# The recurrent unit's input is turned, copied and split ahead of a window of the graph step instead of behind it

## The reference, cut to what matters

```python
msg = h[edge_src] + relvectors[edge_rel]
red = jax.ops.segment_sum(msg, edge_dst, num_segments=h.shape[0])
gi = red @ w_ih.T + b_ih
gh = h @ w_hh.T + b_hh
r = sigmoid(i_r + h_r);  z = sigmoid(i_z + h_z)
n = tanh(i_n + r * h_n)
new = (1.0 - z) * n + z * h
```

## Time and profile before

| | us |
|---|---|
| Median of 3 runs | 3483.4 |
| Lowest and highest | 3481.09, 3487.05 |
| The profiled execution, whole | 3481.69 |
| Its span, first to last instruction | 3480.1 |
| First layer's windows and steps | about 160 to 1620 of the span |
| Mean granted PE clock, share of 2.4 GHz | 0.781 |

### The profile page before, as it was taken

The page is one execution under the profiler, slowest core; times in us unless marked ns, Lnnn a source line. Parts: engine busy times, 40 slices in busy tenths (PEclk is TensorE's granted clock), DMA queues, the critical chain, the costliest instruction groups (busy, mean ns, idle before and its releaser), DMA issues. The chain is left out here.

```text
span 3480.1 us, 54363 instructions
## 1 busy us (share of the span) xinstructions
PE 2374.7 (68%) x13318; PEld 1809.5 (52%) x13319; DVE 1521.8 (44%) x3970; ACT 779.9 (22%) x1414; POOL 1854.4 (53%) x2044
## 2 busy tenths in 40 slices
PE   1278777778677777645577766555543799999991
PEld 1155454545455444524355544433322799999991
DVE  5543443443444443422466554432321454554545
ACT  1222222222222221202101100000000344454440
POOL 0263433443645676771777777777775344444440
PEclk7578788888888888756678766666655899999996
DMA  5331211211222233331433333333332222222116
GB/s 139 97 86 45 61 55 55 61 57 52 85 73 77 79 107 98 100 104 34 114 114 115 113 108 108 108 110 106 106 107 78 86 68 65 68 66 64 45 44 230
DMA packets 157909, 303.68 MB, mean 87 GB/s; under 512 B 47365, under 2 KB 91816, under 8 KB 157752
## 3 DMA queue, kind: packets, MB, share of 16 engines
q0 software_dynamic: 85984, 234.74, 23.2%
q1 hardware_dynamic: 40876, 36.11, 3.4%
q10 hardware_dynamic: 30892, 31.40, 2.8%
HBM read 261.73 MB, written 40.39 MB: 87 GB/s over the span
## 5 line engine op out<-in xcount | busy, mean ns | idle before, releaser
L743 POOL DMA_INDIRECT rows<-table,srcT x1568 | 1552.8, 990 | 910.1 <-issue 463.1
L811 PE MATMUL bank<-rows,onehot 128*128 x3904 | 700.2, 330 | 537.6 <-POOLq L736 403.1
L811 PEld LDWEIGHTS bank<-rows,onehot 128*128 x3904 | 427.4, 109 | 801.4 <-issue 653.5
L772 DVE SCALAR_TENSOR_TENSOR onehot<-iota_row,tbase,dstT 128x512 f16 x488 | 366.2, 752 | 625.9 <-issue 332.9
L1752 PE MATMUL bank<-xe_high,W_high 128*128 128x256 f32 x864 | 252.0, 292 | 30.2 <-DVE xe_low L1830 29.9
L1802 ACT ACTIVATE hid<-bank,b 128x256 f32<-128x256 f32 x432 | 181.2, 471 | 345.6 <-PE bank L1754 345.5
L1838 DVE TENSOR_TENSOR hid_low<-hid,hid_high 128x512 fp32r<-128x512 f32 x216 | 149.6, 693 | 234.4 <-ACT hid_high L1806 234.4
L1753 PE MATMUL bank<-xe_low,W_high 128*128 128x256 f32 x864 | 250.2, 290 | 0.0
L1754 PE MATMUL bank<-xe_high,W_low 128*128 128x256 f32 x864 | 249.9, 289 | 0.0
L1752 PE MATMUL bank<-W_high,hid_high 128*128 128x256 f32 x864 | 248.4, 287 | 0.0
L1754 PE MATMUL bank<-W_high,hid_low 128*128 128x256 f32 x864 | 244.0, 282 | 0.0
(11 more groups left out here) (338 smaller groups left out, 3598.3 us busy)
## 6 DMA issues: line engine op xcount, KB each, us to landing
rows<-table,srcT POOLq DMA_INDIRECT x1568, 2.7
W<-in_L_ffn_W_dram SPq DMA_DIRECT2D x14, 1024.0 KB, 7.5
y<-results ACTq DMA_DIRECT2D x12, 1024.0 KB, 10.3
x_res<-in_x_dram SPq DMA_DIRECT2D x1, 6144.0 KB, 43.8
out_dram<-x_res SPq DMA_DIRECT2D x12, 512.0 KB
table<-part ACTq DMA_DIRECT2D x11, 512.0 KB, 3.2
normal<-xn ACTq DMA_DIRECT2D x11, 512.0 KB, 3.4
table<-part SPq DMA_DIRECT2D x6, 512.0 KB, 2.9
```

Of the source, the lines that this page charges most:

```text
L743: nc.gpsimd.indirect_dma_start(out=rows[:, k % (M * U), 0:ROW], out_offset=None, in_=q.table, in_offset=bass.IndirectOffsetOnAxis(srcT[:, ...
L772: last = nc.vector.scalar_tensor_tensor(onehot[:, ds(slot, U), :], iota_row[:, :].unsqueeze(1).to_broadcast([P, U, P]), base, dstT[:, ds(k ...
L811: last = nc.tensor.matmul(acc[:, 0:cols], hot, ring_rows[:, ds(row0 + (s * q.pitch + at), cols)], start=False, stop=False, skip_group_chec ...
```

## The change

The first three bullets of d1 move to the end of d4 of the group ahead, on each of the three engines. For group 0 they stay in d1. On PE the transposes stand behind the last L1012 and before window 3. On ACT the copies to `t_high` stand behind the last copy of d4 and before the square root. On DVE the subtraction stands behind the last L207 and before the one-hots. Nothing is added or removed: same instructions, tiles and semaphores. The copies to `hT` stay in d1.

```diff
-        def pe_d1(pe, g, w):
-            n = w * P
-
+        def pe_d0(pe, g, w):
             pe.wait_ge(S["h4_ready"], g + 1)
             for c in range(C):
                 for i in range(w):
                     last = nc.tensor.transpose(bank[c][:, i * P:(i + 1) * P], h4_in[:, i, c * P:(c + 1) * P], ident[:, :])
             last.then_inc(S["hT_ps"], 1)
+
+        def pe_d1(pe, g, w):
+            n = w * P
+
+            if isinstance(g, int) and g == 0:
+                pe_d0(pe, 0, w)
...
                 l3(a2_low, 1 + pair, eW3[0][:, pair, :], False, pair == 1)
-
-        def act_d1(act, g, w):
+            if not (isinstance(g, int) and g == LAST):
+                pe_d0(pe, g + 1, size(g + 1))
+
+        def act_d0(act, g, w):
             n = w * P
             act.wait_ge(S["hT_ps"], g + 1)
             for c in range(C):
                 last = nc.scalar.activation(t_high[:, c, 0:n], bank[c][:, 0:n], ACT.Copy)
             last.then_inc(S["hT_high"], 1)
...
+            if not (isinstance(g, int) and g == LAST):
+                act_d0(act, g + 1, size(g + 1))
             ln_sqrt(act, S["x2_var"], S["x2_std"], g, w, scaled=True)
...
             chain.begin(g)
-            dve_low(dve, g, w, t_low, t_high, 0, 1, "hT_high", "hT_low")
+            if isinstance(g, int) and g == 0:
+                dve_low(dve, 0, w, t_low, t_high, 0, 1, "hT_high", "hT_low")
...
             ln_apply(first_tile(g), w).then_inc(S["h2_ready"], 1)
             chain.end()
+            if not (isinstance(g, int) and g == LAST):
+                dve_low(dve, g + 1, size(g + 1), t_low, t_high, 0, 1, "hT_high", "hT_low")
```

More of the change, by code:

```diff
@@ L1040, in act_d1 @@
             last.then_inc(S["hT_high"], 1)
+        def act_d1(act, g, w):
+            n = w * P
+            if isinstance(g, int) and g == 0:
+                act_d0(act, 0, w)
             act.wait_ge(S["ct_ps"], g + 1)
```

## The result

The changed kernel takes 3440.2 us in the median of four runs (3435.27 to 3446.88), the kernel before 3484.2 us beside it. A second pair, further down, gives 0.9886 (0.9868 to 0.9904).

The account below looks back on a forecast made before the run. The chain of steps on PE, DVE and ACT, not POOL's gather, bounds groups 2 to 11. Per group 2.6 - 0.9 = 1.7 us, over ten groups 17 us, from 3483.4 to 3466 us; the range leaving out 2 in 10 is 3455 to 3479.

Parts of the forecast that it names:

- The root: ACT's copies stand before the square root at the end of d4: root 0.2 us late, bounds 0 and 0.9.
- that group's zero: Group 1, like groups 0, 12 and 13, was forecast to gain about zero.
- the clock's term: Products from instruction 10 in d1: half clock for 5 us after PE's wait, giving back 0.8 to 0.9 us a group.
- That gives back 0.8 to 0.9 us: In d1, the block from instruction 10 takes 16.8 us instead of 16.03, against 2.6 us gained before it.
- PE has then waited some 4.5 us in one piece: Ahead of instruction 10 in d1, PE's wait for `red_low` was to be as long as before the change.
- the hand-over: DVE's last one-hot to instruction 10 in d1(6): 5.35 us instead of 8.32, with 0.3 added for hand-overs and register work.
- the 0.4 that I had allowed: PE's transposes stand before window 3: PE reaches its first product at most 0.4 us later, range -0.7 to +0.4.
- The rule of the Trainium skill that I set against the change: Waits between bursts of matmuls put PE back to half clock, each burst paying anew; without it the sum would be 26 us.
- the clock stays full: Rival, chance 0.05: PE's ten products ahead of the wait keep the clock up; 4.05 us a group, 3443 us.
- The one-hots are held back: Rival, chance 0.15: DVE doesn't take the subtractions ahead, one-hots come 0.65 to 1.29 us later; 3474 us.
- slower: Rival, chance 0.08: register work starts only behind the subtraction, one-hots 2.31 us late; 1.4 us lost in ten groups, 3497 us.
- The gain is absorbed: Rival, chance 0.12: what follows d1 ends at its old time, or the copies cost 0.9 us; within 7 us, 3480.

Follow-up runs that it names:

- i1_after: The changed kernel with no edit, run again on an undisturbed chip against the kernel before: 3442.3 us against 3481.1, ratio 0.9886.
- g2_wait_sub: The changed kernel with DVE waiting for its moved subtraction to end ahead of the one-hots: 3465.6 us, ratio 0.9958 to the kernel before.
- the shift: The kernel before with four more semaphore increments on DVE ahead of window 3's one-hots; on an undisturbed chip 3473.1 us against 3481.1, ratio 0.9984.
- g3_fill_before: The kernel before with twelve filler products on PE ahead of the wait for `t_low`, groups 2 to 11: 3474.2 us against 3479.1, ratio 0.9992.

## Why the prediction failed in size and held in direction

**Right.** The reading of the stage: DVE's subtraction behind the one-hots and the turn was what PE waited for. The subtraction is taken ahead in its new place, and the first one-hot is 0.13 us late, forecast 0.15. Behind the last one-hot 3.2 us are saved on average, forecast 2.97. The root is 0.12 us late per group, forecast 0.2; in group 1, which I had left out, it is 2.5 us late and eats the 2.7 us that instruction 10 gains there, so that group's zero holds.

**Wrong: the clock's term.** *"That gives back 0.8 to 0.9 us"* per group, 9 us in all. The step that failed is *"PE has then waited some 4.5 us in one piece"*. From the start of instruction 9 to that of 10 it was 0.4 to 0.5 us in groups 1, 2 and 11, 1.9 to 2.2 in 3, 5 and 10, 3.1 to 3.4 in 6, 7 and 9, and 5.4 and 4.5 only in 4 and 8. Behind the first six the products took 14.6 us, behind the others 16.1, 16.8 and 17.3. Before, it was 14.9 to 16.3 in ten groups. So the term is a gain of 2 us where a loss of 9 was forecast. Of the 23 us by which groups 1 to 11 gained more than forecast in the first trace, 11 are this term, 7.9 the one-hots and 5.2 the stretch behind the last one-hot, and the root takes 1.7 back. Three causes made the pause shorter than I had it: the one-hots were done sooner, the hand-over was 0.4 shorter, and PE came to its first product 0.65 us later behind the residual sum, at the far end of the 0.4 that I had allowed and past it. I took d1(6) for all groups, although the number of one-hots, and with it the pause, differs from group to group.

The rule of the Trainium skill that I set against the change (TensorE: Matmul & The Clock Gate, HAM oscillation - how this bites in real kernels) is told there of waits longer than the bursts between them, and I had applied it as if every pause paid. The trace agrees with it as it stands there. The ten products ahead of instruction 10 start within 2.2 us; behind the five waits longer than that (2.7 to 5.0 us idle) the clock was partly half, behind the six shorter ones it was full. The second trace (i1_after) has the same five and the same six. The price hung on the pause that was left, 9.5 us in sum, and was 11.6 us before.

**Missed: the one-hots.** 7.9 us, in no term, bound or rival. I took the 1.66 us between two one-hots of window 3 for their own pace, though the trace of before had 1.39 to 1.46 us for the same loop in the windows 0 to 2 of each turn and in groups 1 and 2. Why window 3 was slow, and why the changed list isn't, stays open; it isn't the gathers beside it.

**Missed: what is no part of the change.** 8.7 us up to the first group's residual sum in the profiled pair, 7.3 of them the clock's draw. The range of a single profiled execution should have had it.

**The hand-over.** 5.35 us forecast, 4.95 to 5.3 measured; the 0.3 that I added for hand-overs wasn't there. Over the ten groups the saving is 32.2 us for 29.7; group 1 adds 2.7.

The rivals: *the clock stays full* had 3443 us, close to what came, but by a clock that is full in all groups, and that isn't what happened. It is the right number for the wrong reason. *The one-hots are held back* and *slower* are decided by g2_wait_sub: the delay would be 2.35 us or more, and even then the kernel stands at 3465.6 us and not at 3497, because the one-hots keep their faster pace and the clock takes back less than 1.9 us in all groups but group 10 (2.3). *The gain is absorbed*: no, end of products to the next residual sum is unchanged to 0.4 and 1.9 us in sum (single groups by up to 0.9 and 1.7 us).

## What to carry to other kernels

Before work is moved on a shared engine, ask what it will stand in front of, what that engine can take ahead there, and whether something else in the row can step back instead: two copies on ACT were worth 16 us without any of this change, and writing the one-hots where their engine idles, with the root first, 34 us more on top of the changed kernel in groups 1 to 11. Don't take a price from one group of a loop whose groups differ in size; make the table for all of them, and mark each stretch of the clock by the pause ahead of it. Look whether a loop runs at another pace elsewhere in the same trace before its pace is taken as given; this one had 1.40 us in three windows and 1.65 in the fourth, and that went away with any edit of the instruction list ahead of it that was tried. A gain or loss of this size belongs into the range. And an experiment that comes out as forecast can still leave a rival: the shift moved the list as well as the phase.

## What was not expected of the hardware

- A gather that starts 0.14 to 0.24 us behind a one-hot takes 1.33 to 1.43 us instead of 0.95, and doesn't slow DVE: the next one-hot comes after 1.45 us (window 0 of before, nine groups). What they contend for no run here shows.
- The same loop of DVE has one-hots 1.65 us apart in one of its four copies in the hardware loop and 1.40 in the other three. A few more instructions ahead of the slow copy make it 1.40 as well.
- The turn of a hardware loop stands 2.9 to 3.3 us on DVE, and 4.1 us of register work precede a run of one-hots. Six instructions are taken ahead while it goes on, as the Trainium skill has it (Advanced Engine Details and Errata, Engine Queue Depths: 8 for VectorE); no run shows whether eight would be.
- The same code of the first group runs at half or at full clock, 15.6 or 8.3 us for its 72 products, from one execution to the next.
- Twelve filler products that end 1.9 us before a pause does, with another pause of 1.3 us behind, don't hold the clock (g3_fill_before, d1(6)).
